# Turning the probabilities of one query tile by 32x32 VectorE transposes and a DRAM scratch

## The chip, the cores and the metric

The kernel runs on one core of a Trainium2 chip. The metric is the device time in microseconds of one execution. A core has a matrix engine (TensorE, PE in the profile; its weight loads are shown as PEld), a vector engine (VectorE, DVE), an activation engine (ScalarE, ACT), GpSimd (POOL) and SyncE (SP), which here only issues DMA transfers. Each engine works through its own instructions in order and waits on semaphores that the others raise.

## The reference

```python
xn = layernorm(x)                                   # x: 4 x 512 x 256
s = attention(xn, Wq, bq, Wk, bk, Wv, bv, Wo, bo, gamma, beta)
g = silu(ffn(xn, w_gate_up, w_down))                # gated MLP, 1024 inner
out = x + s * g

# attention: 16 heads of 128, 4 key-value heads, causal
scores = einsum('blhe,bmhe->bhlm', Q, K) / sqrt(128) + mask
attn = softmax(scores)
ctx = einsum('bhlm,bmhe->blhe', attn, V)
y = gelu(ctx @ Wo + bo)
r = xn + y
s = (r - mean(r)) * rsqrt(var(r) + 1e-5) * gamma + beta
```

Everything is float32.

## The kernel before

There are 4 rows (b), each of 512 tokens in 4 query tiles of 128, and 16 heads in 4 groups of 4 that share one key-value head (kv). Every float32 product is done in three passes over a high and a low part of each operand: ScalarE writes the rounded high part (`hi`), VectorE subtracts it from the source to get the low part (`lo`), and TensorE multiplies lo by hi, hi by lo and hi by hi (`product`, L949).

The first part (to about 165 us) is the feed-forward net of all rows. Then come 16 segments, one for each row and key-value head. A segment handles four units, one for each query tile from tile 3 down to tile 0. The order of TensorE's work in a segment is written out by hand:

```python
SEGMENT = """
s1.0 t3.0 o s1.1 t3.1 s1.2 p3.0 t3.2 s1.3 s0.0 p3.1 t3.3 s0.1 p3.2 s0.2
t2.0 s0.3 p3.3 t2.1 K p2.0 o t2.2 Q0 Q1 Q2 p2.1
t1.0 p2.2 t1.1 S3.0 Q3 p1.0 S3.1 o p1.1
t0.0 S3.2 S3.3 o S2.0 S2.1 S2.2 p0.0 S2.3
"""
```

Here s1.2 is the score product of query tile 1 for head 2 of the group. t2.1 is the turning of the probabilities of query tile 2 against key tile 1: four TensorE transposes of 128x128, one for each head (`transposes`, L1048), into `probsT_ps`. p2.1 is the product of these turned probabilities with the values (`values`), which sums into `ctx_ps`; o is the output product with Wo of the unit that is ready (`output`). K and Q0 to Q3 are the projections of the next key-value head, and capital S a score product for the next segment. Query tile t has t + 1 key tiles, so tile 1 has two turnings, t1.0 and t1.1, and a segment has ten.

What the others do between these words follows from the same order (`scalar_steps`, `vector_steps`), with lags. For a score s: VectorE scales, masks and takes the least (`tensor_tensor_reduce`, L900), ScalarE takes the exponential in place with the row's sum (L692), VectorE inverts the sum (L907), GpSimd multiplies (L561, the semaphore `probs_made`). For a turning t: ScalarE copies PSUM into `pT_hi` (L698) and VectorE writes `pT_lo` (L804); there are two such pairs, used in turn. After the last p of a unit ScalarE writes `cT_hi` with the bias (L702) and VectorE `cT_lo` (L822), which the unit's o reads; VectorE then adds the output to `y` (L916).

The segment of the last key-value head of a row (ROW_SEGMENT) has four value projections V3 to V0 more, V3 between Q0 and Q1, V2 between S3.1 and the next o. In the first segment of the next row the tail of the row before is done on the side (gelu on ScalarE, statistics and norm on VectorE, the rest on GpSimd). The very last segment has an order of its own.

SyncE's queue in this part is nearly empty: for each row it loads `x_b` and `g_b`, waits for the finished row (`out_made`) and stores it.

Of the kernel before, what the change touches and what calls it, by code (L numbers as in the profile page):

```python
# [28 lines left out]
P = 128  # L29
# [11 lines left out]
PASSES = ((0, 1), (1, 0), (0, 0))  # L41


PIECE = 2048
# [58 lines left out]
PAIRS_OF_KV = T * (T + 1) // 2  # L103
PAIRS = KV * PAIRS_OF_KV
SCORES_ALL = UNITS * G
RING_BANKS = 4
# [89 lines left out]


def behind(steps, lag, i):
# [18 lines left out]

def vector_steps(steps):


    steps = list(steps)
    for i in range(len(steps) + 1):
# [12 lines left out]


def build(nc, x, wq, wk, wv, wo, wgu, wd, bqkv, rows, ident_in, mask_in, g_scratch, out):
    ctx = ExitStack()
# [62 lines left out]
    v_s = pair("v", [P, T, KV * E])  # L301
    probs = [sb(f"probs{t}", [P, G, (t + 1) * P]) for t in range(T)]
    pT = [pair(f"pT{i}", [P, G * P]) for i in range(2)]
# [24 lines left out]
    y_ps = down_ps[:, 3, 0:D]  # L328

    def transposed(step, end):  # L330
# [21 lines left out]
        sem("scores_done"), sem("masked"), sem("exp_done"), sem("inv_made"), sem("probs_made"))  # L352
    probsT_done, probsT_hi, probsT_split = sem("probsT_done"), sem("probsT_hi"), sem("probsT_split")
    ctx_done, ctx_hi, ctx_split = sem("ctx_done"), sem("ctx_hi"), sem("ctx_split")
    y_done, y_added = sem("y_done"), sem("y_added")
# [71 lines left out]
    def _(sp):  # L427
# [48 lines left out]
    def _(pool):  # L476
# [76 lines left out]

        def steps(b, order, ends=()):

            for step in order:
                if step[0] == "s":
                    _, u, g = step
                    pool.wait_ge(inv_made, b * SCORES_ALL + u * G + g + 1)
                    p = probs[tile_of(u)][:, g, :]  # L560
                    nc.gpsimd.tensor_tensor(p, p, inv[:, u % UNITS, g:g + 1].to_broadcast([P, (tile_of(u) + 1) * P]),  # L561
                                            ALU.mult).then_inc(probs_made, 1)
                behind_word(ends, works, b, step)
# [7 lines left out]
        for kv in range(1, KV):  # L571
            steps(B - 1, segment(kv, last=kv == KV - 1))

# [23 lines left out]
    def _(act):  # L597
# [66 lines left out]
        def steps(b, order, ends=(), end=False):  # L664
            for step in scalar_steps(order):
# [21 lines left out]
                elif step[0] == "s":  # L687

                    _, u, g = step
                    p = probs[tile_of(u)][:, g, :]  # L690
                    act.wait_ge(masked, b * SCORES_ALL + u * G + g + 1)
                    nc.scalar.activation(p, p, ACT.Exp, bias=least[:, u % UNITS, g:g + 1], scale=-1.0,  # L692
                                         accum_out=total[:, u % UNITS, g:g + 1]).then_inc(exp_done, 1)
                elif step[0] == "t":
                    r = pair_index(*step[1:])
                    act.wait_ge(probsT_done, b * PAIRS + r + 1)
                    ps, (hi, _) = transposed(step, end)
                    nc.scalar.activation(hi[:], ps, ACT.Copy).then_inc(probsT_hi, 1)  # L698
                elif step[0] == "p" and step[2] == tile_of(step[1]):
                    act.wait_ge(ctx_done, b * UNITS + step[1] + 1)  # L700
                    h = H + KV + kv_of(step[1]) % KV
                    nc.scalar.activation(cT[0][:], ctx_ps, ACT.Identity, bias=bias[:, h:h + 1]).then_inc(ctx_hi, 1)  # L702
                behind_word(ends, {"gelu": gelu}, b, step)
# [17 lines left out]
    def _(dve):  # L721
# [76 lines left out]
        def low_part(step, b, end):  # L798

            if step[0] == "t":  # L800
                r = pair_index(*step[1:])
                dve.wait_ge(probsT_hi, b * PAIRS + r + 1)
                ps, (hi, lo) = transposed(step, end)
                nc.vector.tensor_tensor(lo[:], ps, f32(hi[:]), ALU.subtract).then_inc(probsT_split, 1)  # L804
            elif step[0] == "v":
# [4 lines left out]
            elif step[0] in "kq":  # L810
                ps = ring_ps[banks[step][0]]
                kv = step[1] % KV
                dve.wait_ge(proj_hi, b * PROJ_ALL + proj_index(step) + 1)
                h = H + kv if step[0] == "k" else step[2] * KV + kv
                hi, lo = kT if step[0] == "k" else qT[step[2]]
                nc.vector.scalar_tensor_tensor(lo[:], ps, bias[:, h:h + 1], f32(hi[:]),  # L816
                                               ALU.add, ALU.subtract).then_inc(proj_split, 1)
            else:
                dve.wait_ge(ctx_hi, b * UNITS + step[1] + 1)
                hi, lo = cT  # L820
                h = H + KV + kv_of(step[1]) % KV
                nc.vector.scalar_tensor_tensor(lo[:], ctx_ps, bias[:, h:h + 1], f32(hi[:]),  # L822
                                               ALU.add, ALU.subtract).then_inc(ctx_split, 1)

# [60 lines left out]

        def steps(b, order, ends=(), row_ends=(), end=False):

            of = banks_last if end else banks
            for step in vector_steps(order):
                if step[0] == "masked":  # L890
# [5 lines left out]

                    dve.wait_ge(scores_done, b * SCORES_ALL + n + 1)
                    nc.vector.memset(total[:, u % UNITS, g:g + 1], 0.0)

                    nc.vector.tensor_tensor_reduce(  # L900
                        out=probs[t][:, g, :], in0=ps[:, 0:(t + 1) * P],
                        in1=mask[:, (T - 1 - t) * P:], scale=-SCALE, scalar=BIG, op0=ALU.add, op1=ALU.min,
                        accum_out=least[:, u % UNITS, g:g + 1]).then_inc(masked, 1)
# [24 lines left out]

        steps(0, segment(-1, text=FIRST))
        steps(0, segment(-1, text=AHEAD))  # L930
        steps(0, segment(0))
        for b in range(B - 1):
            for kv in range(1, KV):
                steps(b, segment(kv), ((low_of(kv + 1, "k"), xn_again),) if kv == KV - 1 else ())
            steps(b, segment(KV), row_ends=ROW_END_DVE)
        for kv in range(1, KV - 1):
            steps(B - 1, segment(kv))
        steps(B - 1, segment(KV - 1, last=True), ((("masked", LAST + T - 1, 0), xn_again),), end=True)
        tile_output(LAST + 1)
# [5 lines left out]
    def _(pe):  # L945
# [92 lines left out]
        def transposes(b, u, j, end):  # L1038
            r = pair_index(u, j)
            if j == 0:  # L1040
                pe.wait_ge(probs_made, b * SCORES_ALL + (u + 1) * G)
# [5 lines left out]
            for g in range(G):  # L1047
                last = nc.tensor.transpose(ps[:, g * P:(g + 1) * P],  # L1048
                                           probs[tile_of(u)][:, g, j * P:(j + 1) * P], ident[:])
            last.then_inc(probsT_done, 1)  # L1050

        def values(b, u, j, end):
# [10 lines left out]
            if j == tile_of(u):  # L1063
                last.then_inc(ctx_done, 1)

        def output(b, u):
# [107 lines left out]
```

## Time and profile before

| what | value |
|---|---|
| median of 3 runs | 715.47 us (715.37 to 715.48) |
| time of the profiled execution | 716.74 us |
| its span, first to last instruction | 714.9 us |
| granted TensorE clock, mean | 0.989 |
| busy: PE / PEld / DVE / ACT / POOL | 671.6 / 585.2 / 480.0 / 433.2 / 279.7 us |
| TensorE transposes (L1048) | 624, in 156 groups of four |
| DMA, mean over the span | 28 GB/s |

The times of instructions come from the one profiled execution. Matmuls overlap each other, so the mean length of one says less than the distance from one start to the next; the chain of work that ended last shows such distances. A line of a group of instructions gives busy time in all and the mean of one, and then the idle time of the engine just before them with what ended it.

### The profile page before, as it was taken

The page shows a single profiled execution, that of the slowest core. Times are in us where ns is not written, and L with a number is a line of the kernel's source. Part 1 is how long each engine was busy: PE and PEld are TensorE (multiplying, and loading weights), DVE is VectorE, ACT ScalarE, POOL GpSimd, SP SyncE. Part 2 cuts the span into 40 slices and gives each one's busy share as a digit, 9 for nine tenths or more (in the row PEclk, how much of TensorE's full clock was granted, in tenths as well). Part 3 has the DMA queues.
Part 4 walks back from the last instruction along what each step waited for, and adds up shares of the span by engine and source line. Part 5 has one row for each costly group of instructions (what it writes and reads, how often), then busy time and mean ns, then how long its engine had stood idle before and what let it go on. Part 6 is the DMA issues. An engine that isn't in the chain of part 4 may idle for free.

```text
span 714.9 us, 11581 instructions
## 1 busy us (share of the span) xinstructions
PE 671.6 (94%) x3968; PEld 585.2 (82%) x3968; DVE 480.0 (67%) x1620; ACT 433.2 (61%) x1011; POOL 279.7 (39%) x328
## 2 busy tenths in 40 slices
PE   1889999999999999999999999999999999999982
PEld 1778888888888888897888888888888897888872
DVE  6764433334776777777868776786768677867777
ACT  3423232326767677668767675867767677767661
POOL 2599100000524324146815242484425146715234
PEclk9799999999999999999999999999999999999998
DMA  8334000002000000000110000002000000200000
GB/s 275 119 129 136 1 29 0 30 0 85 5 1 1 1 0 1 1 1 1 56 34 2 1 1 0 2 1 89 1 1 1 1 1 1 89 1 2 1 1 29
DMA packets 14503, 20.31 MB, mean 28 GB/s; under 512 B 752, under 2 KB 12144, under 8 KB 14192
## 3 DMA queue, kind: packets, MB, share of 16 engines
q1 hardware_dynamic: 13328, 14.37, 6.1%
q0 software_dynamic: 1120, 5.24, 2.2%
q8 instruction: 31, 0.51, 0.3%
q14 instruction: 24, 0.20, 0.1%
HBM read 15.41 MB, written 4.19 MB: 27 GB/s over the span
## 4 chain that ended last, share of the span: by engine, by line
PE 86%; DVE 7%; ACT 4%; issue 1%; DMA 1%; SPq 0%; DVEq 0%; ACTq 0%
PE bank L949 30%; PE down_ps L949 28%; PE down_ps L1048 8%; PE down_ps L987 6%; PE bank L974 6%; PE bank L976 6%; DVE cT_lo L822 2%; PE bank L1035 2%; ACT cT_hi L702 2%; DVE hidT_lo L766 1%; DMA raw<-in_wgu 1%; DVE pT_lo L804 1%; DVE xnT_lo L751 1%; ACT L655 1%; ACT res L655 0%
## 5 line engine op out<-in xcount | busy, mean ns | idle before, releaser
L561 POOL TENSOR_TENSOR probs<-probs,inv 128x512 f32<-128x512 f32 (+3 forms) x256 | 180.7, 720 | 385.0 <-DVE inv L907 384.9
L692 ACT ACTIVATE probs<-probs,least 128x512 f32<-128x512 f32 (+3 forms) x256 | 142.2, 558 | 40.5 <-DVE least L900 36.8
L900 DVE CUSTOM_DVE_ANT_0 probs<-bank,mask 128x512 f32<-128x512 f32 (+3 forms) x256 | 121.2, 486 | 12.1 <-issue 12.0
L804 DVE TENSOR_TENSOR pT_lo<-down_ps,pT_hi 128x512 fp32r<-128x512 f32 x156 | 107.1, 687 | 20.0 <-ACT pT_hi L698 15.4
L698 ACT ACTIVATE pT_hi<-down_ps 128x512 fp32r<-128x512 f32 x156 | 92.5, 593 | 33.1 <-PE down_ps L1048 31.1
L1048 PE MATMUL down_ps<-ident,probs 128*128 128x128 f32 x624 | 93.4, 272 | 0.0
L1048 PEld LDWEIGHTS down_ps<-ident,probs 128*128 128x128 f32 x624 | 75.5, 140 | 12.4
L949 PE MATMUL down_ps<-wo_lo,cT_hi 128*128 128x256 f32 x256 | 73.7, 288 | 6.0 <-DVE cT_lo L822 6.0
L816 DVE SCALAR_TENSOR_TENSOR qT_lo<-bank,bias,qT_hi 128x512 fp32r<-128x512 f32 x64 | 47.5, 750 | 43.5 <-ACT qT_hi L685 43.5
L949 PE MATMUL down_ps<-pT_lo,v_hi 128*128 128x512 f32 x156 | 67.8, 435 | 5.6 <-DVE cT_lo L822 4.2
L949 PE MATMUL down_ps<-wo_hi,cT_lo 128*128 128x256 f32 x256 | 72.0, 281 | 0.0
L949 PE MATMUL down_ps<-wo_hi,cT_hi 128*128 128x256 f32 x256 | 71.9, 281 | 0.0
L949 PE MATMUL bank<-kT_lo,qT_hi 128*128 128x512 f32 (+2 forms) x192 | 70.0, 364 | 0.0
L822 DVE SCALAR_TENSOR_TENSOR cT_lo<-down_ps,bias,cT_hi 128x512 fp32r<-128x512 f32 x64 | 48.0, 750 | 31.4 <-ACT cT_hi L702 30.3
L949 PE MATMUL bank<-kT_hi,qT_hi 128*128 128x512 f32 (+2 forms) x192 | 64.9, 338 | 0.0
L949 PE MATMUL bank<-kT_hi,qT_lo 128*128 128x512 f32 (+2 forms) x192 | 64.6, 336 | 0.0
L612 ACT ACTIVATE gate<-bank 128x512 f32<-128x512 f32 x32 | 19.2, 600 | 72.3 <-PE bank L974 72.3
L949 PE MATMUL down_ps<-pT_hi,v_hi 128*128 128x512 f32 x156 | 61.5, 394 | 0.0
L949 PE MATMUL down_ps<-pT_hi,v_lo 128*128 128x512 f32 x156 | 61.3, 393 | 0.0
L949 PEld LDWEIGHTS down_ps<-wo_lo,cT_hi 128*128 128x128 f32 x256 | 48.1, 188 | 13.6 <-DVE cT_lo L822 12.2
L702 ACT ACTIVATE cT_hi<-down_ps,bias 128x512 fp32r<-128x512 f32 x64 | 44.1, 689 | 23.6 <-PE down_ps L949 22.1
L762 DVE TENSOR_TENSOR hid<-gate,bank 128x512 f32<-128x512 f32 x32 | 22.0, 687 | 52.8 <-ACT gate L612 52.8
(139 smaller groups left out, 1547.6 us busy)
## 6 DMA issues: line engine op xcount, KB each, us to landing
x_row<-in_x SPq DMA_DIRECT2D x4, 512.0 KB, 6.8
raw<-in_wgu SPq DMA_DIRECT2D x4, 512.0 KB, 6.1
raw<-in_wq POOLq DMA_DIRECT2D x2, 1024.0 KB, 5.1
raw<-in_wo POOLq DMA_DIRECT2D x2, 1024.0 KB, 6.2
g_scratch<-g_out SPq DMA_DIRECT2D x4, 512.0 KB, 2.9
x_b<-in_x SPq DMA_DIRECT2D x4, 512.0 KB, 3.7
g_b<-g_scratch SPq DMA_DIRECT2D x4, 512.0 KB, 4.7
out<-res SPq DMA_DIRECT2D x3, 512.0 KB, 2.9
```

Of the source, the lines that this page charges most:

```text
L561: nc.gpsimd.tensor_tensor(p, p, inv[:, u % UNITS, g:g + 1].to_broadcast([P, (tile_of(u) + 1) * P]), ALU.mult).then_inc(probs_made, 1)
L692: nc.scalar.activation(p, p, ACT.Exp, bias=least[:, u % UNITS, g:g + 1], scale=-1.0, accum_out=total[:, u % UNITS, g:g + 1]).then_inc(exp_ ...
L698: nc.scalar.activation(hi[:], ps, ACT.Copy).then_inc(probsT_hi, 1)
L702: nc.scalar.activation(cT[0][:], ctx_ps, ACT.Identity, bias=bias[:, h:h + 1]).then_inc(ctx_hi, 1)
L804: nc.vector.tensor_tensor(lo[:], ps, f32(hi[:]), ALU.subtract).then_inc(probsT_split, 1)
L816: nc.vector.scalar_tensor_tensor(lo[:], ps, bias[:, h:h + 1], f32(hi[:]), ALU.add, ALU.subtract).then_inc(proj_split, 1)
L822: nc.vector.scalar_tensor_tensor(lo[:], ctx_ps, bias[:, h:h + 1], f32(hi[:]), ALU.add, ALU.subtract).then_inc(ctx_split, 1)
L900: nc.vector.tensor_tensor_reduce(out=probs[t][:, g, :], in0=ps[:, 0:(t + 1) * P], in1=mask[:, (T - 1 - t) * P:], scale=-SCALE, scalar=BIG, ...
L949: ins = nc.tensor.matmul(dst, left[a], right[c], start=first and i == 0, stop=last and i == len(PASSES) - 1)
L974: gate_mm = nc.tensor.matmul(gate_ps[c % 2], wgu_s[left][:, k, c * P:(c + 1) * P], tokens[right], start=first_pass, stop=last_pass)
L976: up_mm = nc.tensor.matmul(up_ps[c % 2], wgu_s[left][:, k, F + c * P:F + (c + 1) * P], tokens[right], start=first_pass, stop=last_pass)
L1048: last = nc.tensor.transpose(ps[:, g * P:(g + 1) * P], probs[tile_of(u)][:, g, j * P:(j + 1) * P], ident[:])
```

## The change

In 15 of the 16 segments (all but the last) query tile 1's probabilities are no longer turned by TensorE. The tile's probabilities are kept in blocks of 32 columns, so that the four heads of one block lie side by side. VectorE turns each 32x32 block of the whole [128, 1024] tensor in place in one instruction, placed in its order where t2.1 stands. SyncE then writes the tensor to a DRAM scratch (512 KB), waits for it, and reads it back in 8 transfers of 64 KB (32 partitions each, in pieces of 512 bytes) into a new SBUF tensor `moved`, in which the blocks stand where a full transpose would have them. ScalarE and VectorE make `pT_hi` and `pT_lo` from `moved` and not from PSUM; ScalarE waits for all 8 transfers. Because the columns are then in the order block, head, place, `cT_hi` is written through a rearranged view, and `cT_lo` in four instructions of 128 columns. Among the waits that are added are one of ScalarE for p2.1 (`pT_read`) and one of VectorE for the scratch write of the segment before.

```diff
+BLOCK = 32
+BLOCKS = P // BLOCK
+TURNED = 1
+TURN_AT = "t2.1"
...
 def vector_steps(steps, kv, end):
+        if step == turn:
+            yield "x", kv * T + T - 1 - TURNED
         if step[0] == "o":
             yield step
...
+    moved = sb("moved", [P, TURNED + 1, BLOCKS, G * BLOCK])
...
+        probs_blocks = probs[TURNED][:].rearrange("p (k n) -> p k n", n=G * BLOCK)
+        scratch_of = p_scratch.rearrange("(i a) (j q) n -> q a j i n", i=BLOCKS, q=BLOCKS)
+
+        def turn(b, kv):
+            n = b * KV + kv
+            sp.wait_ge(blocks_made, n + 1)
+            sp.dma_start(p_scratch, probs_blocks).then_inc(blocks_out, 16)
+            if n:
+                before = kv - 1 if kv else KV - 1
+                sp.wait_ge(probsT_split, (b - (kv == 0)) * PAIRS + pair_index(before * T + T - 1 - TURNED, TURNED) + 1)
+            sp.wait_ge(blocks_out, 16 * n + 16)
+            for q in range(BLOCKS):
+                for j in range(TURNED + 1):
+                    sp.dma_start(moved[q * BLOCK:(q + 1) * BLOCK, j], scratch_of[q, :, j]).then_inc(moved_in, 16)
+            sp.wait_ge(moved_in, (n + 1) * BLOCKS * (TURNED + 1) * 16)
+
         for b in range(B):
+            if b:
+                turn(b, 0)
+                sp.wait_ge(out_made, 2 * b)
+                sp.dma_start(out_v[b - 1], res[:]).then_inc(out_stored, 16)
+                sp.wait_ge(out_stored, 16 * b)
             sp.dma_start(x_b[:], x_v[b]).then_inc(x_b_in, 16)
             sp.dma_start(g_b[:], g_v[b]).then_inc(g_b_in, 16)
-            if b < B - 1:
-                sp.wait_ge(out_made, 2 * b + 2)
-                sp.dma_start(out_v[b], res[:]).then_inc(out_stored, 16)
-                sp.wait_ge(out_stored, 16 * b + 16)
+            for kv in range(1 if b else 0, KV - 1 if b == B - 1 else KV):
+                turn(b, kv)
...
+                    if is_turned(u, end):
+                        act.wait_ge(moved_in, (b * KV + kv_of(u) + 1) * BLOCKS * (TURNED + 1) * 16)
+                        if j == 0:
+                            act.wait_ge(pT_read, b * KV + kv_of(u) + 1)
+                        else:
+                            act.wait_ge(ctx_done, b * UNITS + u)
+                        nc.scalar.activation(pT[r % 2][0][:], moved_pair(j), ACT.Copy).then_inc(probsT_hi, 1)
...
+                if is_turned(step[1], end):
+                    hi, lo = pT[r % 2]
+                    nc.vector.tensor_tensor(lo[:], moved_pair(step[2]), f32(hi[:]), ALU.subtract).then_inc(probsT_split, 1)
...
+                if is_turned(step[1], end):
+                    for q in range(BLOCKS):
+                        last = nc.vector.scalar_tensor_tensor(
+                            by_heads(lo[:], True)[:, :, q], as_heads(ctx_ps, True)[:, :, q], bias[:, h:h + 1],
+                            by_heads(f32(hi[:]), True)[:, :, q], ALU.add, ALU.subtract)
+                    last.then_inc(ctx_split, 1)
...
+                elif step[0] == "x":
+                    dve.wait_ge(probs_made, b * SCORES_ALL + (step[1] + 1) * G)
+                    p = probs[TURNED][:]
+                    nc.vector.transpose(p, p).then_inc(blocks_made, 1)
...
         def transposes(b, u, j, end):
             r = pair_index(u, j)
+            if is_turned(u, end):
+                return
```

## Rows read from the trace of the kernel before

**Rows 1.** Page, part 1: busy time and share of each engine.
```profile
PE 671.6 (94%) x3968; PEld 585.2 (82%) x3968; DVE 480.0 (67%) x1620; ACT 433.2 (61%) x1011; POOL 279.7 (39%) x328
```

**Rows 2.** Busy time by segment: an ordinary one, a ROW_SEGMENT, a row's first.
```profile
224.30:256.00 31.70, 31.46 (x195) 27.61 (x194) 23.12 (x88) 22.34 (x57) 11.31 (x16) 1.00 0.01 2
287.70:325.00 37.30, 37.30 (x222) 32.63 (x221) 26.55 (x95) 25.82 (x61) 11.27 (x16) 1.00 0.00 1
325.00:357.30 32.30, 30.93 (x189) 26.97 (x189) 25.72 (x102) 24.16 (x60) 24.49 (x26) 1.00 0.10 30
```

**Rows 3.** Chain that ended last, 226 to 259 us: start, length, what.
```profile
233.50 0.44 PE down_ps L1048 x4
...
234.63 0.44 PE down_ps L1048 x4
```

**Rows 4.** TensorE's timeline in the same segment: p1.0, p1.1, S3.3 and o.
```profile
236.98 0.39 PE L949 MATMUL down_ps<-pT_lo,v_hi 128*128 128x512 f32 x1
...
240.25 0.39 PE L949 MATMUL down_ps<-pT_hi,v_hi 128*128 128x512 f32 x1
...
242.07 0.39 PE L949 MATMUL bank<-kT_hi,qT_hi 128*128 128x512 f32 x1
242.31 0.28 PE L949 MATMUL down_ps<-wo_lo,cT_hi 128*128 128x256 f32 x1
```

**Rows 5.** VectorE's timeline, same segment.
```profile
224.98 0.75 DVE L822 SCALAR_TENSOR_TENSOR cT_lo<-down_ps,bias,cT_hi 128x512 fp32r<-128x512 f32 x1 [0.24 <-ACT cT_hi L702]
225.85 0.69 DVE L804 TENSOR_TENSOR pT_lo<-down_ps,pT_hi 128x512 fp32r<-128x512 f32 x1
...
241.40 0.75 DVE L822 SCALAR_TENSOR_TENSOR cT_lo<-down_ps,bias,cT_hi 128x512 fp32r<-128x512 f32 x1 [0.99 <-ACT cT_hi L702]
242.07 0.15 DVE L907 RECIPROCAL inv<-total 128x1 f32<-128x1 f32 x1
```

**Rows 6.** GpSimd's timeline: the last product of tile 1 there.
```profile
223.45 0.61 POOL L561 TENSOR_TENSOR probs<-probs,inv 128x256 f32<-128x256 f32 x1 [0.46 <-DVE inv L907]
```

**Rows 7.** ScalarE's timeline, same segment.
```profile
233.97 0.60 ACT L698 ACTIVATE pT_hi<-down_ps 128x512 fp32r<-128x512 f32 x1 [0.18 <-PE down_ps L1048]
...
240.68 0.69 ACT L702 ACTIVATE cT_hi<-down_ps,bias 128x512 fp32r<-128x512 f32 x1 [0.18 <-PE down_ps L949]
```

**Rows 8.** Groups of instructions with shapes kept apart.
```profile
L804 DVE TENSOR_TENSOR pT_lo<-down_ps,pT_hi 128x512 fp32r<-128x512 f32 x156 | 107.1, 687 | 20.0 <-ACT pT_hi L698 15.4
...
L900 DVE CUSTOM_DVE_ANT_0 probs<-bank,mask 128x512 f32<-128x512 f32 x64 | 42.8, 686 | 0.0
...
L766 DVE TENSOR_TENSOR hidT_lo<-hid,hidT_hi 128x512 fp32r<-128x512 f32 x32 | 34.8, 1087 | 25.3 <-ACT hidT_hi L616 25.3
...
L900 DVE CUSTOM_DVE_ANT_0 probs<-bank,mask 128x256 f32<-128x256 f32 x64 | 26.0, 419 | 6.2 <-issue 6.2
...
L616 ACT ACTIVATE hidT_hi<-hid 128x512 fp32r<-128x512 f32 x32 | 20.2, 632 | 25.8 <-DVE hid L762 25.8
```

**Rows 9.** SyncE's timeline of DMA issues.
```profile
0.74 0.99 SPq L434 DMA_DIRECT2D x_row<-in_x  x2
...
4.84 3.75 SPq L431 DMA_DIRECT2D raw<-in_wd  x2
...
351.77 0.38 SPq L465 DMA_DIRECT2D out<-res  x1
354.71 0.37 SPq L461 DMA_DIRECT2D x_b<-in_x  x1
355.13 0.51 SPq L462 DMA_DIRECT2D g_b<-g_scratch  x1
```

**Rows 10.** DMA issues: KB of one, median us from issue to landing.
```profile
x_b<-in_x SPq DMA_DIRECT2D x4, 512.0 KB, 3.7
g_b<-g_scratch SPq DMA_DIRECT2D x4, 512.0 KB, 4.7
...
out<-res SPq DMA_DIRECT2D x4, 128.0 KB, 1.7
```

**Rows 11.** Row's first segment: VectorE's timeline around t2.1.
```profile
326.38 0.73 DVE L822 SCALAR_TENSOR_TENSOR cT_lo<-down_ps,bias,cT_hi 128x512 fp32r<-128x512 f32 x1
328.57 0.69 DVE L804 TENSOR_TENSOR pT_lo<-down_ps,pT_hi 128x512 fp32r<-128x512 f32 x1 [1.46 <-ACT pT_hi L698]
```

More of the change, by code:

```diff
@@ L195, in pair_index, with transposes_before, is_turned @@
     return kv_of(u) * PAIRS_OF_KV + sum(tile + 1 for tile in range(tile_of(u) + 1, T)) + j
+def transposes_before(r, end):
+    kv, i = divmod(r, PAIRS_OF_KV)
+    turned = PAIRS_OF_KV - (TURNED + 1) * (TURNED + 2) // 2
+    return kv * TRANSPOSED // KV + (i if end or i < turned else i - (TURNED + 1))
+def is_turned(u, end):
+    return tile_of(u) == TURNED and not end
 def behind(steps, lag, i):
@@ L215, in scalar_steps, with vector_steps @@
             yield steps[i]
-def vector_steps(steps):
+def vector_steps(steps, kv, end):
     steps = list(steps)
+    turn = None if end or kv < 0 else next(segment(kv, text=TURN_AT))
     for i in range(len(steps) + 1):
@@ L232, in vector_steps, with build @@
         yield from (("inv", *x[1:]) for x in behind(steps, INVERSE_LAG, i))
+        if step == turn:
+            yield "x", kv * T + T - 1 - TURNED
         if step[0] == "o":
             yield step
-def build(nc, x, wq, wk, wv, wo, wgu, wd, bqkv, rows, ident_in, mask_in, g_scratch, out):
+def build(nc, x, wq, wk, wv, wo, wgu, wd, bqkv, rows, ident_in, mask_in, g_scratch, p_scratch, out):
     ctx = ExitStack()
@@ L301, in build @@
     v_s = pair("v", [P, T, KV * E])
-    probs = [sb(f"probs{t}", [P, G, (t + 1) * P]) for t in range(T)]
+    probs = [sb(f"probs{t}", [P, G * (t + 1) * P]) for t in range(T)]
+    moved = sb("moved", [P, TURNED + 1, BLOCKS, G * BLOCK])
     pT = [pair(f"pT{i}", [P, G * P]) for i in range(2)]
@@ L328, in build, with probs_row, as_blocks, as_heads @@
     y_ps = down_ps[:, 3, 0:D]
+    def probs_row(u, g, end):
+        t = tile_of(u)
+        if is_turned(u, end):
+            return probs[t][:].rearrange("p (k g m) -> p k g m", g=G, m=BLOCK)[:, :, g, :]
+        return probs[t][:].rearrange("p (g n) -> p g n", g=G)[:, g, :]
+    def as_blocks(ap, turned):
+        return ap.rearrange("p (k m) -> p k m", m=BLOCK) if turned else ap
+    def as_heads(ap, turned):
+        return ap.rearrange("p (q g m) -> p g q m", q=BLOCKS, g=G) if turned else ap
+    def by_heads(ap, turned):
+        return ap.rearrange("p (g q m) -> p g q m", q=BLOCKS, g=G) if turned else ap
+    def moved_pair(j):
+        return moved[:, j].rearrange("p q n -> p (q n)")
     def transposed(step, end):
@@ L552, in _, with steps @@
         works = {"residual": residual, "root": root, **{f"out{i}": out_piece(i) for i in range(8)}}
-        def steps(b, order, ends=()):
+        def steps(b, order, ends=(), end=False):
             for step in order:
@@ L571, in _ @@
         for kv in range(1, KV):
-            steps(B - 1, segment(kv, last=kv == KV - 1))
+            steps(B - 1, segment(kv, last=kv == KV - 1), end=kv == KV - 1)
         def tile_root_of(t):
@@ L689, in steps @@
                     _, u, g = step
-                    p = probs[tile_of(u)][:, g, :]
+                    p = probs_row(u, g, end)
                     act.wait_ge(masked, b * SCORES_ALL + u * G + g + 1)
@@ L884, in tile_output, with steps @@
             nc.vector.tensor_tensor(r, r, x_b[:, t, :], ALU.add).then_inc(tile_out_dve, 1)
-        def steps(b, order, ends=(), row_ends=(), end=False):
+        def steps(b, kv, order, ends=(), row_ends=(), end=False):
             of = banks_last if end else banks
-            for step in vector_steps(order):
+            for step in vector_steps(order, kv, end):
                 if step[0] == "masked":
@@ L897, in steps @@
                     dve.wait_ge(scores_done, b * SCORES_ALL + n + 1)
+                    if t == TURNED and g == 0 and b * KV + kv_of(u):
+                        dve.wait_ge(blocks_out, (b * KV + kv_of(u)) * 16)
                     nc.vector.memset(total[:, u % UNITS, g:g + 1], 0.0)
                     nc.vector.tensor_tensor_reduce(
-                        out=probs[t][:, g, :], in0=ps[:, 0:(t + 1) * P],
-                        in1=mask[:, (T - 1 - t) * P:], scale=-SCALE, scalar=BIG, op0=ALU.add, op1=ALU.min,
+                        out=probs_row(u, g, end),
+                        in0=as_blocks(ps[:, 0:(t + 1) * P], is_turned(u, end)),
+                        in1=as_blocks(mask[:, (T - 1 - t) * P:], is_turned(u, end)), scale=-SCALE, scalar=BIG, op0=ALU.add, op1=ALU.min,
                         accum_out=least[:, u % UNITS, g:g + 1]).then_inc(masked, 1)
@@ L927, in low_of @@
             return "low", (step[0], kv, *step[1:])
-        steps(0, segment(-1, text=FIRST))
-        steps(0, segment(-1, text=AHEAD))
-        steps(0, segment(0))
+        steps(0, -1, segment(-1, text=FIRST))
+        steps(0, -1, segment(-1, text=AHEAD))
+        steps(0, 0, segment(0))
         for b in range(B - 1):
             for kv in range(1, KV):
-                steps(b, segment(kv), ((low_of(kv + 1, "k"), xn_again),) if kv == KV - 1 else ())
-            steps(b, segment(KV), row_ends=ROW_END_DVE)
+                steps(b, kv, segment(kv), ((low_of(kv + 1, "k"), xn_again),) if kv == KV - 1 else ())
+            steps(b, KV, segment(KV), row_ends=ROW_END_DVE)
         for kv in range(1, KV - 1):
-            steps(B - 1, segment(kv))
-        steps(B - 1, segment(KV - 1, last=True), ((("masked", LAST + T - 1, 0), xn_again),), end=True)
+            steps(B - 1, kv, segment(kv))
+        steps(B - 1, KV - 1, segment(KV - 1, last=True), ((("masked", LAST + T - 1, 0), xn_again),), end=True)
         tile_output(LAST + 1)
@@ L1039, in transposes @@
             r = pair_index(u, j)
+            if is_turned(u, end):
+                return
             if j == 0:
@@ L1064, in values @@
                 last.then_inc(ctx_done, 1)
+            elif tile_of(u) == TURNED + 1 and j == tile_of(u) - 1:
+                last.then_inc(pT_read, 1)
         def output(b, u):
@@ L1170 @@
     out = nc.dram_tensor("out", (B, L, D), F32, kind="ExternalOutput").ap()
-    build(nc, *args, g_scratch, out)
+    p_scratch = nc.dram_tensor("p_scratch", (P, BLOCKS * (TURNED + 1), G * BLOCK), F32, kind="Internal").ap()
+    build(nc, *args, g_scratch, p_scratch, out)
     r = run_bass_kernel_spmd(nc, [arrays], core_ids=[0])
```

36 lines of the change are left out of this document (23 added, 13 removed).

## The prediction

> **What bounds the kernel now.** I began with the page's busy times [rows 1]: TensorE is busy 94% of the span, VectorE 67%, ScalarE 61%. An average hides stages, so next came busy time by segment [rows 2]. An ordinary segment lasts 31.70 us and TensorE is busy for 31.46 of them; VectorE has 8.6 us and ScalarE 9.4 us free. In the attention part time is therefore TensorE's, and a change is worth what it takes off TensorE's queue, less what it makes that queue wait. The chain of waits says what one turning takes there: a group of four transposes sets the end back by 0.44 us [rows 3]. Then the timelines of the engines in one ordinary segment [rows 4 to 7] say how long before its use each piece is ready, which the averages can't say.
>
> **What is removed.** t1.0 and t1.1 leave TensorE's queue: 2 x 0.44 = 0.88 us a segment, 15 segments, 13.2 us. The share of the 624 transposes that goes is 120.
>
> **The new way from the block transpose to p1.0.** This decides. I time it from the row's own places in the ordinary segment, and ask when pT of t1.0 is ready against when TensorE wants it.
>
> TensorE starts p1.0 at 236.98 [rows 4]; without the two turnings in front it would come there at 236.1.
>
> The block transpose x stands after cT_lo of unit 3 (started 224.98) and before pT_lo of t2.1 (225.85) [rows 5]. An operation like this cT_lo lets its successor start 0.67 us after it (241.40 to 242.07) [rows 5], so x starts at 225.65. It waits for GpSimd's last product of tile 1, which ended at 223.45 + 0.61 = 224.06 [rows 6]: no wait, unless GpSimd's four products grow by 1.6 us together through the 32-column pieces. From 225.65 to 236.1 are 10.45 us, and in them must fit:
>
> - x itself, 1024 columns. No row has it. The masking operation takes 419 ns for 256 columns and 686 for 512 [rows 8]: 1.04 ns a column and 0.15 fixed, so 1.22 us. From above: with both operands in SBUF the subtraction takes 1087 for 512 against 687 with one in PSUM [rows 8], 2.1 ns a column with nothing fixed, which gives 2.2 us. x has one operand and is like the first, so I take 1.22; from below it is that less the fixed part, 1.07.
> - The scratch write, 512 KB with 4 KB a partition: from the issue of `out<-res` to the next issue behind its wait 354.71 - 351.77 = 2.94 us [rows 9], the same size and form.
> - Seven issues before the last read. x_b to g_b are 0.42 us apart; at the kernel's start seven issues take 4.84 - 0.74 = 4.10, or 0.59 each [rows 9]. So 2.9 to 4.1; I take 0.5 each, 3.5.
> - The last read, issue to landing. 128 KB out land in 1.7 us, 512 KB in (x_b) in 3.7. g_b, issued 0.42 after x_b, lands at 0.42 + 4.7 = 5.12, so 512 KB more take 1.4 us [rows 9, 10]; 64 KB in are then 3.7 - 7/8 x 1.4 = 2.5. From 1.7 to 2.5; I take 2.1, in the middle, since it is as small as the one and a read like the other.
> - Signals between engines, two at about 0.1: 0.2.
> - ScalarE's pT_hi from SBUF, 632 ns as hidT_hi, not 593; VectorE's pT_lo from two SBUF operands, 1087 and not 687 [rows 8]; with gaps 1.85.
>
> Sum 1.22 + 2.94 + 3.5 + 2.1 + 0.2 + 1.85 = 11.8 us against 10.45: TensorE waits 1.36 us at p1.0. ScalarE meets the wait first: its order has t1.0 at 233.97 [rows 7] and stands there until the data are in at 235.6. Behind it are cT_hi of unit 2, t1.1, Q3's parts; TensorE wants cT for o only 1.4 us after p1.0 starts, and Q3's low part later still, so by the same lengths these arrive behind p1.0's delay and add nothing. VectorE is later by 0.4 us for each pT_lo, into gaps that it has there (0.99 us idle before the cT_lo at 241.40 [rows 5]).
>
> **cT of the turned unit.** p1.1's last pass starts at 240.25, cT_hi at 240.68, cT_lo at 241.40, o at 242.31 [rows 4, 5, 7]; between are only t0.0, S3.2 and S3.3, whose last pass starts at 242.07 and takes 0.23 to the next start, as such passes do. So TensorE is free at 242.30 and cT_lo ends at 242.15: about 0.1 us of cover is left after the signal. Four pieces of 128 columns: the 0.75 us operation costs its successor 0.67, of which 0.53 are 512 columns at 1.04 ns, so a piece costs about 0.27, the last seen at 0.35: 3 x 0.27 + 0.35 = 1.16 us, 0.41 more than 0.75. With waits rounded, o starts 0.37 us later in each turned segment. Below, if views of 4 x 32 run faster: nothing; above: four full fixed parts, 0.65.
>
> **Costed at nothing.** x on VectorE: 1.2 us ahead of pT_lo of t2.1, whose p2.1 comes 7 us later, and of kT_lo, used 8 us later; without those gaps it would cost 1.2 a segment. The masking, exponential and scaling of tile 1 through 32-column pieces: same columns; each could cost up to a tenth of a us, in front of x's 1.6 us of slack. SyncE's queue: the row's store and the loads of x_b and g_b now stand behind turn(b, 0), which ends at about 10 us after t2.1, before out_made comes in that segment, and the next turn is 20 us off. The wait for the scratch write of the segment before is 20 us old. pT_read is p2.1, which ends before the old t1.0 did.
>
> **The sum.** An ordinary segment: -0.88 + 1.36 + 0.37 = +0.85. A row's first segment is like it: x would start 0.67 behind 326.38 and even finds 1.46 us of idleness [rows 11]. That makes 12 segments, +10.2. The three ROW_SEGMENTs have V3 between x and p1.0: four V's make 37.30 - 31.70 = 5.6 [rows 2], one 1.4, which covers the 1.36; each gives -0.88 + 0.37 = -0.51, together -1.5. Sum +8.7 us on the profiled execution's 716.74: 725.4. The median of the runs is 1.27 below that execution: 724.2.
>
> Beside this, a rule of the Trainium skill (DMA: Bandwidth & Descriptors, Rules for kernel authors) says that splitting a transfer over disjoint partitions brings nothing, as the parts share the same 16 engines; it speaks against eight reads. If parts cost together just what one transfer costs, they would land together 3.7 us after the first issue [rows 10], not 5.6; rival A takes this up. For x, the Vector Engine (DVE) Microarchitecture Reference (3.8) gives the transposing front end one element per cycle and lane; at 0.96 GHz (Trainium Kernel Development and Optimization, NeuronCore Architecture) that is an estimate of 1.07 us and speaks against the upper bound.
>
> **Rivals.**
>
> A, the data come in time: the eight reads land as one transfer in 3.7 us. For it: 512 KB move in that time in the x_b row. Against it: SyncE's issues are at least 0.42 us apart, so the last is issued 2.9 us after the first. The wait falls by 1.9, to nothing; 15 x -0.51 = -7.7, so 707.8. It decides from a wait under 0.5 us. Chance 0.14. If the wait falls between 0.5 and 0.75 us, the two sides cancel: about 715.5, chance 0.07.
>
> B, the forecast: a wait of ScalarE for the reads, 0.75 to 2 us: 717 to 733. Chance 0.62.
>
> C, x takes 2.2 us, or the 512-byte pieces make the reads as much later: the wait is 2.35, ordinary segments +1.84, the ROW_SEGMENTs +0.45: 22.1 + 1.4 = 23.5, so 739. Against it: one operand. Chance 0.13.
>
> D, VectorE becomes the bound: each us added counts, 1.22 + 0.8 + 0.41 - 0.88 = 1.55 by 15 = 23, so 739. Against it: 8.6 us free in a segment, 2.4 added. Chance 0.04.
>
> **Numbers.** Faster or slower by under 0.2% (1.4 us) can't be told from no change. Faster 0.14, same 0.07, slower 0.79. One us on the way from x to p1.0 is worth 12 us or more, which sets the range. With issues at 2.9 and a landing of 1.7 the wait is 0.36 and the time 712; with 4.1 and 2.5 it is 2.36 and the time 739, which I cut to 737, as all bounds together are unlikely. The range 712 to 737 leaves out most of A and half of C and D, some 2 in 10. Within B alone 717 to 733.
>
> **What would show it.** L1048 at 504 instructions, not 624. A wait of ScalarE at `pT_hi<-moved` ended by a DMA, 12 times over 1 us, 3 times near nothing; behind it TensorE's p1.0 waiting for `pT_lo`, about 1.4 us. Issue to issue of the reads 0.5, last landing 2.1, x 1.2 us. TensorE waiting some 0.4 us for `cT_lo` before the third o. An ordinary segment of 32.5 us. Wrong it would be by faster issues of small transfers, a slow block transpose, or 32-column pieces slowing GpSimd so that x itself starts late.

## The result, and the profile after

The changed kernel takes 730.75 us (median of 4 runs, 726.84 to 735.33), the kernel before 715.48. The ratio on record is 1.0189, 95% interval 1.013 to 1.0248; like all ratios below it is an estimate from all the runs and not the quotient of the two medians, which is 1.021. The change is slower, by 15.3 us between the medians; whether by more than 2% stays unclear. That is inside the range of 712 to 737 and of the forecast sign, but the forecast cost was 8.7. The four runs spread by 8.5 us, where the four of before spread by 2; in the larger batches of the experiments the kernel before spread by 7 us too.

The profiled execution took 734.03 us, with a span of 732.4. First the lines by shape that the terms of the sum spoke of (busy us, mean ns, idle before):

```profile
L1145 PE MATMUL down_ps<-ident,probs 128*128 128x128 f32 x504 | 75.4, 272 | 0.0
...
L882 DVE TENSOR_TENSOR pT_lo<-moved,pT_hi 128x512 fp32r<-128x512 f32 x30 | 23.0, 766 | 16.8 <-ACT pT_hi L769 16.7
L769 ACT ACTIVATE pT_hi<-moved 128x512 fp32r<-128x512 f32 x30 | 18.7, 625 | 19.3 <-DMA moved<-p_scratch 19.1
L1002 DVE STREAM_TRANSPOSE probs<-probs 128x1024 f32<-128x1024 f32 x15 | 18.5, 1234 | 0.0
L905 DVE SCALAR_TENSOR_TENSOR cT_lo<-down_ps,bias,cT_hi 128x128 fp32r<-128x128 f32 x60 | 16.9, 345 | 14.9 <-ACT cT_hi L778 14.9
```

The turnings are 504 as told, the block transpose takes 1.23 us and waits for nothing, and ScalarE loses 19.1 us waiting for the reads, in 13 waits, 12 of them over 1 us as told. The work on tile 1's probabilities in pieces of 32 columns is no slower: masking 421 ns (419 before), exponential 504 (504), GpSimd's product 613 (613). The chain that ended last, in an ordinary segment (start, us, what), is the way that the prediction priced; it answers to [rows 3 to 7]:

```profile
259.73 1.16 DVE probs L1002
...
260.95 2.62 DMA p_scratch<-probs
...
263.64 0.30 SPq L518
263.94 0.05 issue
263.99 0.43 SPq L518
...
266.83 1.99 DMA moved<-p_scratch
268.81 0.02 issue
268.84 0.64 ACT pT_hi L769
269.48 0.02 issue
269.50 0.69 DVE pT_lo L882
270.19 0.67 DVE cT_lo L910
270.87 0.14 issue
271.00 0.93 PE down_ps L1044 x3
```

Write 2.62, issues 0.47 apart, last read 1.99 from issue to landing: all close to what was priced. But p1.0 does not start after pT_lo; it starts after `cT_lo` of unit 2, at 271.00, and TensorE's own timeline says so too:

```profile
271.00 0.47 PE L1044 MATMUL down_ps<-pT_lo,v_hi 128*128 128x512 f32 x1 [0.74 <-DVE cT_lo L910]
```

That segment and three others by window (busy time of PE, PEld, DVE, ACT, POOL, then granted clock, DMA share, GB/s), against 31.70 and, for a row's first, 30.68 before when cut at the same places (from one `k_first` on ScalarE to the next):

```profile
260.08:292.23 32.15, 31.06 (x185) 26.72 (x185) 24.33 (x92) 22.33 (x56) 11.31 (x16) 1.00 0.10 33
397.90:433.65 35.75, 32.60 (x185) 28.14 (x185) 24.33 (x92) 22.33 (x56) 11.32 (x16) 0.95 0.09 30
331.23:365.40 34.17, 31.62 (x180) 27.32 (x180) 27.08 (x105) 22.26 (x58) 23.05 (x25) 0.95 0.23 77
609.05:640.57 31.52, 30.12 (x181) 25.90 (x180) 26.82 (x105) 22.17 (x58) 22.99 (x25) 1.00 0.25 83
```

The first is an ordinary, undisturbed segment: +0.45. The second is ordinary too, and costs 4.05; the last two are first segments of a row and cost 3.5 and 0.84. Where the clock column says 0.95, TensorE had stood for 2.21 or 2.80 us before p1.0. In the second segment the same chain reads:

```profile
398.77 4.59 DMA p_scratch<-probs
...
410.89 0.93 PE down_ps L1044 x3
411.82 1.06 PE bank L1044 x3
412.88 3.29 PE down_ps L1044 x15
```

The write landed 2 us late, TensorE stood still for 2.80 us before 410.89, and then the same 15 passes (o and p1.1) took 3.29 us instead of the 2.13 of the undisturbed segment. The granted clock was at its lower level for 3.4 us, from 411.94 on. In the segment at 331.23 the write was on time, but the last read was issued 0.25 us late and took 2.84 us to land, against 1.99:

```profile
337.24 2.84 DMA moved<-p_scratch
```

By kind of segment, after less before:

| segments | predicted | measured in the profiled execution |
|---|---|---|
| 9 ordinary | 9 x 0.85 = 7.7 | 10.0: six between 0.45 and 0.84, then 1.15, 1.40, 4.05 |
| 3 first of a row | 3 x 0.85 = 2.6 | 7.8: 3.49, 3.51, 0.84 |
| 3 with V's | 3 x -0.51 = -1.5 | -1.0: 0.04, -0.54, -0.48 |
| ahead of them | 0 | 0.7 |

Together 17.5, the difference of the spans.

### The profile page after: what moved, and what is told of

Read it like the earlier page. It is cut to its first block, busy times and chain, and to the rows that moved or that the text cites. A ratio compares the mean times of both kernels' runs of the same rounds, so it can differ in the third digit from the quotient of the medians.

```text
span 732.4 us, 11595 instructions
## 1 busy us (share of the span) xinstructions
PE 670.9 (92%) x3848; PEld 576.5 (79%) x3848; DVE 505.6 (69%) x1680; ACT 432.9 (59%) x1011; POOL 282.6 (39%) x328
## 3 DMA queue, kind: packets, MB, share of 16 engines
q1 hardware_dynamic: 32768, 30.10, 12.4%
## 4 chain that ended last, share of the span: by engine, by line
PE 57%; DVE 16%; DMA 10%; ACT 8%; SPq 5%; issue 3%; POOL 0%; DVEq 0%; ACTq 0%
PE down_ps L1044 22%; PE bank L1044 14%; PE down_ps L1082 6%; DMA p_scratch<-probs 5%; PE bank L1069 5%; PE bank L1071 5%; SPq L518 5%; DVE cT_lo L910 4%; ACT cT_hi L778 4%; PE down_ps L1145 4%; DMA moved<-p_scratch 4%; DVE cT_lo L905 2%; DVE probs L1002 2%; PE bank L1130 2%; DVE pT_lo L882 2%
## 5 line engine op out<-in xcount | busy, mean ns | idle before, releaser
L885 DVE TENSOR_TENSOR pT_lo<-down_ps,pT_hi 128x512 fp32r<-128x512 f32 x126 | 86.0, 683 | 14.8 <-ACT pT_hi L773 12.0
L773 ACT ACTIVATE pT_hi<-down_ps 128x512 fp32r<-128x512 f32 x126 | 74.6, 592 | 29.3 <-PE down_ps L1145 26.2
L1044 PE MATMUL down_ps<-wo_lo,cT_hi 128*128 128x256 f32 x256 | 76.5, 299 | 7.8 <-DVE cT_lo L910 6.0
L1145 PE MATMUL down_ps<-ident,probs 128*128 128x128 f32 x504 | 75.4, 272 | 0.0
L1145 PEld LDWEIGHTS down_ps<-ident,probs 128*128 128x128 f32 x504 | 60.6, 140 | 8.4
L1044 PEld LDWEIGHTS down_ps<-pT_lo,v_hi 128*128 128x128 f32 x156 | 29.7, 191 | 33.3 <-DVE pT_lo L882 20.8
```

The costliest lines, as they stand in the source:

```text
L1044: ins = nc.tensor.matmul(dst, left[a], right[c], start=first and i == 0, stop=last and i == len(PASSES) - 1)
L1145: last = nc.tensor.transpose(ps[:, g * P:(g + 1) * P], probs_row(u, g, end)[:, j * P:(j + 1) * P], ident[:])
```

## The experiments

Each was timed beside the kernel before on the same chip, and the ratio is to that; the median of before was 715.53 to 716.08 us. Segments are cut from one `k_first` on ScalarE to the next, as above.

**No engine waits for the reads** (`e1_no_dependency`).

```diff
+    still = sb("still", [P, G * P])
...
-                        act.wait_ge(moved_in, (b * KV + kv_of(u) + 1) * BLOCKS * (TURNED + 1) * 16)
...
-                        nc.scalar.activation(pT[r % 2][0][:], moved_pair(j), ACT.Copy).then_inc(probsT_hi, 1)
+                        nc.scalar.activation(pT[r % 2][0][:], still[:], ACT.Copy).then_inc(probsT_hi, 1)
...
-                    nc.vector.tensor_tensor(lo[:], moved_pair(step[2]), f32(hi[:]), ALU.subtract).then_inc(probsT_split, 1)
+                    nc.vector.tensor_tensor(lo[:], still[:], f32(hi[:]), ALU.subtract).then_inc(probsT_split, 1)
```

> The block transpose, the scratch write and the eight reads all stay, but pT of t1.0 and t1.1 is made from a constant SBUF tensor, so no engine but SyncE waits for the reads (the turned probabilities are left out of the result). Theory 1, TensorE is held at p1.0 by the reads, through ScalarE: the wait goes, each turned segment becomes 0.88 us shorter less 0.37 for cT_lo in four pieces, 15 x 0.51 = 7.7 us below before, about 708 us. Rival 2, the 2.4 us added on VectorE set the end: they are all still there, so the time stays near 730. Rival 3, the DMA traffic itself slows the other engines: it stays near 730 too.

712.37 against 716.08, ratio 0.9953 (0.9922 to 0.9985). So the wait is the cost: all of VectorE's work and all DMA traffic are still there. But 3.7 us were won and not 7.7. By windows, an ordinary segment and a row's first:

```profile
255.60:286.80 31.20, 30.85 (x185) 26.78 (x185) 24.28 (x92) 22.24 (x56) 11.31 (x16) 1.00 0.10 34
325.29:356.83 31.54, 30.09 (x180) 25.90 (x180) 27.53 (x105) 22.17 (x57) 23.04 (x25) 1.00 0.25 82
```

The ordinary one is 0.50 shorter, as worked out (0.51). The row's first is 0.86 longer than before even without a wait for the reads, 1.37 more than its share. Its VectorE timeline shows why:

```profile
331.03 2.06 DVE L898 SCALAR_TENSOR_TENSOR qT_lo<-bank,bias,qT_hi 128x512 fp32r<-128x512 f32 x3
333.00 1.66 DVE L883 TENSOR_TENSOR pT_lo<-still,pT_hi 128x512 fp32r<-128x512 f32 x1
334.58 0.74 DVE L911 SCALAR_TENSOR_TENSOR cT_lo<-down_ps,bias,cT_hi 128x512 fp32r<-128x512 f32 x1
335.24 1.10 DVE L883 TENSOR_TENSOR pT_lo<-still,pT_hi 128x512 fp32r<-128x512 f32 x1
```

VectorE has no gap there, and the subtraction with both operands in SBUF takes 1.66 and 1.10 us, where it takes 0.68 in every ordinary segment. On GpSimd the products of the row's tail run at that time:

```profile
331.56 5.95 POOL L614 TENSOR_TENSOR res<-res,rowc 128x512 f32<-128x512 f32 x4
```

The kernel before has the same two side by side, but there the subtraction reads one operand from PSUM. It takes 0.68 us, and GpSimd's four take 5.04:

```profile
334.71 5.04 POOL L548 TENSOR_TENSOR res<-res,rowc 128x512 f32<-128x512 f32 x4
...
336.15 0.68 DVE L804 TENSOR_TENSOR pT_lo<-down_ps,pT_hi 128x512 fp32r<-128x512 f32 x1
```

So the price belongs to two SBUF operands beside this GpSimd work, not to VectorE's load.

**Key tile 0's reads first** (`e2_by_key_tile`).

```diff
-            for q in range(BLOCKS):
-                for j in range(TURNED + 1):
-                    sp.dma_start(moved[q * BLOCK:(q + 1) * BLOCK, j], scratch_of[q, :, j]).then_inc(moved_in, 16)
...
+            for j in range(TURNED + 1):
+                for q in range(BLOCKS):
+                    sp.dma_start(moved[q * BLOCK:(q + 1) * BLOCK, j], scratch_of[q, :, j]).then_inc(moved_in[j], 16)
...
+                        act.wait_ge(moved_in[j], (b * KV + kv_of(u) + 1) * BLOCKS * 16)
```

> The four reads of key tile 0 are issued first, with a semaphore of their own, and ScalarE waits at t1.0 for these alone, at t1.1 for the other four. Theory 1: the last read that t1.0 needs is issued 4 x 0.47 = 1.9 us earlier, so the 1.05 us wait of an undisturbed segment goes, as do the drops of the clock behind the longer ones; only a write that lands more than 0.9 us late still shows. About 709 us, at most 714. Rival 2 (VectorE's load) and rival 3 (traffic): near 730, since neither load changes.

716.21 against 716.08, ratio 1.0003 (0.9978 to 1.0029). An ordinary segment takes 31.20 us, the same as without any dependency, a row's first 31.55. Only the segments with a late write still wait (32.47 for the worst). The four issues in front of t1.0 were the wait of an undisturbed segment. The 709 told was missed: the run without any dependency stayed at 712.37 too, for the three first segments, and the late writes come on top.

**cT in one instruction** (`e3_ct_one`).

```diff
-                    for q in range(BLOCKS):
-                        last = nc.vector.scalar_tensor_tensor(
...
+                nc.vector.scalar_tensor_tensor(lo[:], ctx_ps, bias[:, h:h + 1], f32(hi[:]),
+                                               ALU.add, ALU.subtract).then_inc(ctx_split, 1)
...
+            last = product(by_heads(ctx_ps, turned), [w[:, j, at:at + E] for w in v_s],
+                           [as_heads(w[:], turned) for w in pair_of], j == 0, j == tile_of(u))
```

> The order block, head, place is undone by TensorE's value products, which read pT through a rearranged view, and cT_hi and cT_lo of the turned unit are one plain instruction each, as before. Theory 1 with its term for cT: cT_lo is 0.4 us shorter, 15 x 0.37 = 5.5 us less, about 725 us. If o's wait is hidden behind something else: no change, 731. If the moving operand in pieces of 32 columns is slow, TensorE's 90 passes of p1.0 and p1.1 grow and it is slower than 731.

731.86 against 716.08, ratio 1.023 (1.0185 to 1.0275). The 725 told was missed, and the time shows nothing, since runs differ by 9 us (727.35 to 736.71). The segment does: 31.86 us where it was 32.15, so 0.3 of the 0.37. TensorE's passes over 32-column pieces start 0.23 us apart, as the others do, and cost nothing.

This run also prices the clock. In two of its first segments of a row TensorE stood before p1.0 for 2.21 and 2.19 us, as long as in the change, but no drop of the clock followed. They took 32.36 and 32.34 us, against 34.17 and 34.19. Less the 0.3 for cT, a drop costs 1.5 us.

**The block transpose alone** (`e4_x_alone`): the kernel before with `nc.vector.transpose(spare[:], probs[1]...)` added at t2.1.

> The kernel before with only the block transpose added, out of place into an unused tensor, at the place where the change has it; TensorE turns all tiles as before. Theory 1: it lies in VectorE's idle time, no change, 715.5 (at most +1). Rival 2, VectorE's load is on the path: 15 x 1.24 = 18.6, about 734.

715.26 against 716.08, ratio 0.9989 (0.9965 to 1.0014). It is hidden, in the row's first segments too: they stay at 30.68.

**Both edits** (`e5_both`), the second and third run's in one kernel.

> Key tile 0's reads first with a semaphore of their own, and cT of the turned unit in one plain instruction each. In the two separate runs an ordinary segment went from 32.15 to 31.20 us by the first and from 32.15 to 31.85 by the second. Theory 1, the two are separate waits of TensorE one behind the other: 30.9 us a segment, 15 x 0.3 = 4.5 us under the run with the first alone, 711 to 712 us. Rival, the second was only noise of the scratch write: no different from the first alone, 716.

709.11 against 715.53, ratio 0.9905 (0.9869 to 0.994), better than before by 6.4 us, and the best of all. An ordinary segment takes 30.80 us, a row's first 31.15.

**Not in a row's first segment** (`e6_not_in_row_first`).

```diff
-    return tile_of(u) == TURNED and not end
+    return tile_of(u) == TURNED and not end and kv_of(u) % KV != 0
```

> As the run with both edits, but the segments with a row's first key-value head keep TensorE's turning: 11 turned segments. Theory: in those three, VectorE is the bound (they cost 31.54 us against 30.68 before even without any wait for the reads), so each gets back 0.86 us and more, the very first segment gives up 0.8: 11 segments at 0.8 less than before, 8.8 us, less some 2 us for late scratch writes: 708 to 709 us. If the loss there is not VectorE's but the store and loads on SyncE's queue, it stays at 711 to 712.

712.2 against 715.53, ratio 0.9949 (0.9916 to 0.9981). The three segments did return to 30.68 us, from 31.15; the very first lost 0.9 as told. The 708 to 709 told was missed. By the windows the three segments regain only 1.4 us, since with both edits they stood at 31.15 and not at 31.54, and the very first gives 0.9 back; in the profiled execution late writes made segments of 31.49, 31.50 and 32.07 us, and ScalarE waited 1.52 us in the last turned one. The intervals of this run and the last overlap. The time of 712 is the one told for the other theory, that the row's store and loads on SyncE's queue cost the time in these segments. The run without a dependency speaks against it: its chain through such a segment runs over VectorE from 325.4 to 336.3 us without a step on SyncE or of a DMA.

**Sixteen reads** (`e7_sixteen_reads`): each read cut in two of 16 partitions.

> The change with each of the eight reads cut in two halves of 16 partitions: the same bytes, 8 more issues at 0.47 us. If the bytes or the landing set the arrival: no change, 731. If the issues do, t1.0 is 3.8 us later in each of 15 segments: 57 us, 788. If besides each wait of TensorE over 2 us is followed by some 4 us at a lower clock, as behind the longest waits of the change (o took 3.28 us and not 2.12), another 1.2 us a segment: 18 us, 805.

809.63 against 715.53, ratio 1.1299 (1.1254 to 1.1345). An ordinary segment takes 37.59 us, 5.4 more than with eight. The arrival is 3.87 later (ScalarE starts t1.0 at 12.63 us behind k_first, not 8.76), which leaves 1.6 for the clock. The trace shows TensorE after one of these waits (the fourth row is S3.1's first pass, the fifth and sixth are o's first two):

```profile
285.08 0.73 PE L1046 MATMUL down_ps<-pT_lo,v_hi 128*128 128x512 f32 x1 [4.61 <-DVE cT_lo L912]
285.61 0.63 PE L1046 MATMUL down_ps<-pT_hi,v_lo 128*128 128x512 f32 x1
286.04 0.63 PE L1046 MATMUL down_ps<-pT_hi,v_hi 128*128 128x512 f32 x1
286.47 0.63 PE L1046 MATMUL bank<-kT_lo,qT_hi 128*128 128x512 f32 x1
...
287.75 0.42 PE L1046 MATMUL down_ps<-wo_lo,cT_hi 128*128 128x256 f32 x1
287.96 0.42 PE L1046 MATMUL down_ps<-wo_hi,cT_lo 128*128 128x256 f32 x1
...
288.58 0.28 PE L1046 MATMUL down_ps<-wo_hi,cT_lo 128*128 128x256 f32 x1
288.70 0.28 PE L1046 MATMUL down_ps<-wo_hi,cT_hi 128*128 128x256 f32 x1
```

Starts of 512-column passes are 0.43 us apart, where they are 0.23 otherwise, and those of 256 columns 0.21 apart and from 288.58 on 0.12. TensorE is at the lower of its two levels, 1.2 GHz and not 2.4, for 3.4 us after it restarts.

**The turnings kept** (`e8_turnings_kept`): on the kernel with key tile 0's reads first.

```diff
             if is_turned(u, end):
+                pe.wait_ge(probsT_split, b * PAIRS + r - 1)
+                ps = probsT_ps[r % 2]
+                for g in range(G):
+                    nc.tensor.transpose(ps[:, g * P:(g + 1) * P], ident[:], ident[:])
                 return
```

> The kernel with key tile 0's reads first, but TensorE still issues the eight transposes of t1.0 and t1.1 at p1.0's and p1.1's turning places, of the identity, into PSUM that nobody reads. If 0.44 us each is what they cost on the path, an ordinary segment grows from 31.20 to 32.08 us and the time by 15 x 0.88 = 13.2, from 716 to 729. If TensorE's transposes were hidden: 716.

723.18 against 715.53, ratio 1.0116 (1.0063 to 1.0168); the second run had 1.0003. An ordinary segment takes 32.07 us and not 31.20, so 0.87 for two turnings. A row's first stays at 31.53 (31.55 without them) with TensorE busier by 0.87: TensorE is not the bound there. So 12 segments at 0.87 make 10.4 us by the windows and not 13.2. The medians differ by 8.1 (1.0116 less 1.0003). The kept turnings also cover part of a late write: behind one of 3.52 us the segment took 32.06 us, like the others, where without the turnings one of 3.55 made it 31.50 instead of 31.20.

**cT of unit 2 before t1.0** (`e9_ct_before_turning`).

```diff
-t1.0 p2.2 t1.1 S3.0 Q3 p1.0 S3.1 o p1.1
+p2.2 t1.0 t1.1 S3.0 Q3 p1.0 S3.1 o p1.1
```

The same swap is made in ROW_SEGMENT.

> The change with the words t1.0 and p2.2 swapped. TensorE's queue is the same, as it no longer works at t1.0; ScalarE and VectorE make cT of unit 2 before they turn to the data that come back, not behind them. Theory: p1.0 writes ctx_ps and so waits for cT_lo of unit 2 as well, and in the change that stands behind ScalarE's wait for the reads; without it p1.0 waits for pT_lo alone, 0.8 us less in each waiting segment (31.35 us for an ordinary one, not 32.15), and fewer waits pass 2 us: 12 x 0.8 = 9.6, about 721 us. If p1.0 waits only for pT_lo anyway: no change, 731.

725.72 against 716.03, ratio 1.0125 (1.0089 to 1.0161). A little above the 721 told: an ordinary segment takes 31.56 us, 0.6 less than the change, not 0.8. The chain there no longer leads to the reads:

```profile
270.81 0.70 ACT cT_hi L778
271.51 0.03 issue
271.53 0.75 DVE cT_lo L910
272.28 0.61 DVE pT_lo L882
272.89 0.04 issue
272.94 0.96 PE down_ps L1044 x3
```

In this segment ScalarE does not wait for the reads at all; p1.0 now waits for the two VectorE operations after p2.2.

**Both edits and that order** (`e10_both_ct_before`).

> Both edits (key tile 0's reads first, cT in one instruction) and the words t1.0 and p2.2 swapped. An ordinary segment has no wait at p1.0 left (30.80 us), so by the theory only the segments with a late scratch write gain: 0 to 3 us below the 709 of both edits.

713.98 against 716.03, ratio 0.9981 (0.9954 to 1.0008). A miss: every ordinary segment takes 31.15 to 31.18 us, late write or not, against 30.80 for both edits alone. The order frees the kernel of the late writes and puts pT_lo of t1.0 behind cT_lo of unit 2 on VectorE, ahead of p1.0, in every segment.

**Both edits, the block transpose before cT_lo of unit 3** (`e11_both_x_earlier`): `TURN_AT = "p3.3"`.

> Both edits, and the block transpose one step of the order earlier, before cT_lo of unit 3. The data come back 0.9 us earlier, which only late scratch writes can use: 0 to 2 us below 709. If o of unit 3 then waits for the later cT_lo (it has 0.9 us to spare, x takes 1.16), it is slower by up to 0.3 us a segment: 4 us above.

717.61 against 716.03, ratio 1.0007 (0.999 to 1.0024), where at most 713 was told. In the chain of an ordinary segment:

```profile
226.94 1.14 DVE probs L995
228.09 0.64 DVE cT_lo L903
228.73 0.14 issue
228.87 2.36 PE down_ps L1037 x15
```

TensorE's 15 passes at 228.87 are p2.0 and o. Not o but p2.0 waited for cT_lo of unit 3: the first p of each unit overwrites `ctx_ps`, which that cT_lo reads. So 0.8 us a segment, 31.61 against 30.80. In one segment, at 33.27 us, TensorE's clock also fell.

## Why the prediction was right, point by point

**Right: the mechanism, the sign and the gain of the removal.** 0.44 us a turning (0.87 for two, the run with the turnings kept), and a wait of ScalarE for the reads that eats more than that (without the dependency the kernel is faster than before). The block transpose was priced 1.22 and took 1.23, and is hidden, as its run alone shows. Issue spacing 0.5 against 0.47, landing 2.1 against 2.0, write 2.94 against 2.69 from issue to the next issue. Of the rivals, C is out by the durations of x and of the reads, and D (VectorE as the bound in all segments) by the run without a dependency, which kept all of VectorE's work. A failed on its own premise: the issues, not the bytes, set the arrival, as the sixteen reads show (3.87 us for 8 more). Here the Trainium skill (DMA: Bandwidth & Descriptors, Rules for kernel authors) was of use as advice, not as a price: it says that splitting over partitions wins nothing, and the trace adds that each split part costs 0.47 us of SyncE.

**Two errors that cancel in part: the end of the chain.** The step said that after the reads come pT_hi and pT_lo with two SBUF operands at 1087 ns, and then p1.0. The 1087 was the mean of a group of 32 whose median is 693: a few instructions of up to 4.7 us in it spoiled it. In ordinary segments pT_lo takes 0.69. But p1.0 also waits for cT_lo of unit 2, since both use `ctx_ps`; the prediction saw cT_hi and cT_lo held up behind ScalarE's wait, and said that only the o behind p1.0 wanted them. From landing to p1.0 are 271.00 - 268.82 = 2.18 us, against 1.85 priced. And the write and the issues were priced 0.6 us too long: from x to p1.0 are 11.27 us, not 11.8. So the wait costs an undisturbed segment 0.95 us (32.15 less the 31.20 without a dependency) and not 1.36, and the segment is 0.45 longer, not 0.85. That p1.0 really waits for cT_lo of unit 2 is shown by the run with cT first (0.6 us a segment) and by the one with the earlier block transpose (0.8 lost at p2.0 in the same way).

**In part luck: the total.** Twelve segments were priced 0.4 us too dear, 4.8 us together. The three points below, late reads counted with the late writes, had no term in the sum and brought 12.4 us in the profiled execution: 5.9 in ordinary segments and 6.5 in first segments of a row. The time stayed within the range partly because these errors have opposite signs.

**Mis-sized: the row's first segments,** taken as ordinary at +0.85 and measured at 7.8 us for three. The step said that x finds idle time there, which is right; but behind the statistics and the norm VectorE has no gap for a pT_lo that takes 1.1 to 1.7 us. In the run without a dependency the two subtractions grew by 1.4 us together, and such a segment is 0.86 longer than before although two turnings are gone; the third one in the change lost just that (0.84). The other two lost 3.5: about 0.86, 1.2 for TensorE's longer stand (2.2 us against 0.99), and some 1.5 for the clock.

**Missing: the late write.** One duration of a transfer was used as if it were fixed. Most writes end at 2.62 to 2.70 us from issue to next issue, but in the profiled execution five of 15 took 3.2 to 4.7, together 5.1 us longer. The reads vary too: the last one landed in 2.84 us in one segment and in 2.38 in another, where most take 2.0. The spread of the runs is not explained by this: the kernel before has no such write and spread by 7 us as well, and in eight of the ten traces with 15 writes the late ones include the same four (the 2nd, 4th, 7th and 14th). The profiled execution of the block transpose alone has a span 4.2 us longer than before's; all its segments are as long, and the first `k_first` comes 4.5 us later.

**Missing: the clock.** A wait of TensorE was priced at its length. Behind waits of 2.21, 2.80 and 2.19 us the granted clock was at its lower level for 3.4 us, and the 15 passes behind the longest took 3.29 us, not 2.13. Behind 1.4 and 1.6 us it was not, and in the run with cT in one instruction not behind four of 2.2 either. The sum had no term for it. Each drop cost 1.5 us, so the three about 4.5; with the sixteen reads it is some 1.6 us a segment, by subtraction.

**cT in four pieces:** priced 0.37 a segment (its own terms, 0.41 less 0.1 of cover, give 0.31), 0.3 by the run with that edit alone and 0.4 (31.20 to 30.80) on top of the other.

## What to carry to other kernels

A detour through DMA that hides its time only just is priced by its issues and its slowest landing, not by its median: count the issues in front of the first consumer, and give that consumer a semaphore of its own. Before pricing a wait, list everything that is in order behind the waiting engine and every buffer that its results free; here the accumulator's reader mattered as much as the data. And a mean from a group is a price only when its minimum and median agree with it.

## What the runs showed of the hardware

- VectorE's subtraction of 128x512 with both operands in SBUF took 0.68 to 0.69 us in all ordinary segments, as with one in PSUM, and 0.75 to 1.77 us beside GpSimd's row products, which grew as well (5.95 us for the first four in the run without a dependency, 5.04 in the kernel before). The Trainium skill (SBUF — State Buffer, Who interferes with whom) states that a VectorE instruction with two SBUF inputs contends with a GpSimd instruction that reads SBUF; the trace agrees. In the run that keeps TensorE's turning in these segments GpSimd's four take 1.30 us each again. No run here took GpSimd's work away.
- Late scratch writes mostly had a packet of the instruction queue (`q8 instruction`) beside them. For the write at 398.77 (4.66 us) and the one at 260.95 (2.69 us) the DMA view shows:

```profile
q1 hardware_dynamic: 144, 0.52, 29.0%
q8 instruction: 1, 0.02, 1.2%
```

```profile
q1 hardware_dynamic: 144, 0.52, 48.2%
```

  Of the 161 writes in the eleven traces that have them, 50 had such a packet in flight in their first 2.3 us, and 45 of these took 3.0 us or more to the next issue; of the other 111 it was 16. That they fall together is measured, that the one causes the other is not shown.
- A 32-column block transpose of 128x1024 float32 took 1.23 us; 1.22 was worked out from the masking operation, which only passes over its columns. The moving operand of a matmul read in pieces of 32 columns cost TensorE nothing: the passes start 0.23 us apart, as with plain operands.
